# A two-layer kernel (routed experts, then a gated recurrence): fp32 injection of the gate inputs on TensorE, output sum on VectorE, GpSimd left with scaling

## The chip, the cores and the metric

The kernel runs on one NeuronCore of a Trainium2 chip. The metric is the device time of one execution, in microseconds (us). Five engines work side by side: TensorE (PE in the rows, its weight loads PEld), VectorE (DVE), ScalarE (ACT), GpSimd (POOL) and SyncE (SP), which only issues transfers here.

## What is computed

The input x is (2, 1024, 256): B = 2 sequences, T = 1024 steps, D = 256 features. The first layer is a mixture of four experts and a shared branch, the second a gated recurrence over the 1024 steps. Both add to their input.

```python
# layer 1, per expert e (and the shared branch), weights w_be from a small gating network
h = gelu(x @ ew1[e] + eb1[e]);  y = h @ ew2[e] + eb2[e]
out = out + w_be[:, e] * mask[e] * y          # H = 1024 hidden units
x = x + out + shared(x)
# layer 2, with v* = cond @ C_* + b_*
def step(h, xs):                               # 1024 times, each needs the h before it
    z = sigmoid(xzt + h @ U_z + vz)
    r = sigmoid(xrt + h @ U_r + vr)
    hh = tanh(xht + r * h @ U + vh)
    return (1.0 - z) * h + z * hh
x = x + all h                                  # xz, xr, xh = x @ W_z, x @ W_r, x @ W
```

## The kernel before

Everything lies features on partitions (two blocks of 128, KC = 2) and time and batch along the free side. Time is cut into CH = 16 chunks of TC = 64 steps, each chunk into BODIES = 4 bodies of STEPS = 16 steps: 64 bodies, counted n = 0 to 63, with steps t = 0 to 15 in each.

**The recurrence.** One step (`gru_body` on TensorE and on VectorE) goes round three engines. TensorE multiplies the state by the recurrent matrices, cut into fp16 halves (`u_high`, `u_mid`), with the state in fp16 halves as well (`h_parts`, HI and LO): 8 products on HI and 4 on LO for gate R, the same for Z (all at L873). ScalarE takes the tanh of R (`gate_tanh`, L481), VectorE forms r*h in halves (`p_parts`, L684 to L687), TensorE multiplies these for the candidate C (8 and 4 products again), ScalarE takes its tanh, and VectorE's scans (L701 to L705) make the new state, the fp16 HI half first, then LO (L708). The rest of the R products waits for LO.

**The side work.** Layer 1 of later chunks runs on TensorE in two windows of every step: window 0 between the Z products and the C products, window 1 after the C products (`gap_work`). A table (`UNITS`) gives window 0 one unit and window 1 two, and only one to window 1 where t is 7 or 15. A unit is one fp32 product, a weight matrix of 128x128 on 128 columns (`up` L806, `down` L822, `gate_input` L833): two MATMUL records in the trace. Where the table has no unit, `gap_work` issues bf16 products that are not used (L887): one of 256 columns in window 0, two of 512 in window 1. ScalarE applies the gelu (L476), and GpSimd multiplies the result by the expert's weight (`scale_tile`, L298), for which `down` waits.

**The injection.** A PSUM bank per gate holds the inputs of a whole body: at its start `inject` writes the projected inputs of 16 steps (64 columns) into the bank, and the recurrent products add to them. Projected inputs are made by `gate_input` and ScalarE (`input_part`, L491) into `xpart`, fp32. GpSimd then cuts `xpart` into three bf16 parts (`split`, L372 to L379), and `inject` multiplies each on a bf16 identity (L859): three products for a gate. Gate R of body n+1 is injected at the end of body n after window 1 of t = 15, gate Z at t = 0 between R's HI and R's LO products (in other steps three of Z's HI products stand there), gate C at t = 0 ahead of window 0.

```python
def inject(g, last_of_body):
    for i in range(3):
        last = mm(gate_ps[g][:, 0:KC * SC], ident16[:, :],
                  xsplit[:, i, g * KC:(g + 1) * KC, :].rearrange("p k n -> p (k n)"),
                  start=(i == 0), stop=(i == 2), skip_group_check=True)
```

**The output.** At the end of a body VectorE marks it (L712), GpSimd scales the 16 states (L387) and adds the layer's input (`add_body`, L392) into `out_feat`; TensorE transposes the sum to rows in window 1 of t = 1 of the next body (`turn_body`, L854; in body 0 it turns zeros), ScalarE copies them out (L500, after t = 5), SyncE stores.

Of the kernel before, what the change touches and what calls it, by code (L numbers as in the profile page):

```python
# [23 lines left out]
ALU = mybir.AluOpType  # L24
# [4 lines left out]
BF16 = mybir.dt.bfloat16  # L29
I32 = mybir.dt.int32  # L30

P = 128
# [17 lines left out]
def moe_gru_kernel(nc, x, cond, gate_w, gate_b, time_w, time_b, ew1, eb1, ew2, eb2, sw1, sb1, sw2, sb2,  # L50
# [45 lines left out]
    UNITS, GELUS, RESIDUALS, PIECES, FIRST_SPLIT = {}, {}, {}, {}, {}  # L96
    for c in range(CH - 1):
        slots = [(c * TC + s, window) for s in range(TC)
                 for window in ((0, 1) if s % 8 == 7 else (0, 1, 1))]
        for kind, f, i in side_work(c):  # L100
# [13 lines left out]
            if kind == PROJECT:  # L114
                after = at[0] + at[1]
                for m in range(KC):
                    PIECES[after + m] = [(f, i, m, b) for b in range(B)]
                FIRST_SPLIT[after + KC] = f
    FIRST_SPLIT = {max(step for step, g in FIRST_SPLIT.items() if g == f): f for f in range(1, CH)}
# [6 lines left out]
    with ctx:  # L126
# [30 lines left out]
        xrest = sb("xrest", [P, GATES * KC, SC])  # L157
        xsplit = sb("xsplit", [P, 3, GATES * KC, SC], BF16)
        h_hist = sb("h_hist", [P, ROUND, 2 * ST])
        h_true = sb("h_true", [P, KC, SC])  # L160
# [35 lines left out]
        body_mark = sb("body_mark", [P, 1])  # L196
# [35 lines left out]
        pool_passed = sem("pool_passed")  # L232
# [29 lines left out]
        split_ready = sem("split_ready")  # L262
# [7 lines left out]
        body_h = sem("body_h")  # L270
        body_added = sem("body_added")
        h_unscaled = sem("h_unscaled")
# [29 lines left out]
        def _(sp):  # L302
# [6 lines left out]
            sp.sem_inc(out_written, 2 * 16)  # L309

# [12 lines left out]
            def store_body(n):  # L323

                sp.wait_ge(turned_copied, n + 2)
# [14 lines left out]
            sp.wait_ge(out_written, (CH * BODIES + 1) * 2 * 16)  # L340
# [3 lines left out]
        def _(pool):  # L344
# [10 lines left out]
            pool.sem_inc(split_ready, 1)  # L355
            pool.memset(out_feat[:, :, :], 0.0).then_inc(body_added, 1)
            CHAIN0, PER_SPLIT = 1, 3

            def wait_apart(semaphore, value):

                pool.wait_ge(semaphore, value)
                pool.sem_inc(pool_passed, 1)

            def split(c, j):

                n = c * BODIES + j
                chain = n * PER_SPLIT + CHAIN0
                src = xpart[:, c % 2, :, j * SC:(j + 1) * SC]
                if j == 0:
                    pool.wait_ge(xp_ready, (c + 1) * (GATES * KC * B) + 1)  # L370
                wait_apart(injected, n + 1)
                pool.tensor_copy(xsplit[:, 0, :, :], src).then_inc(pool_chain, 1)  # L372
                wait_apart(pool_chain, chain + 1)
                pool.tensor_tensor(xrest[:, :, :], src, xsplit[:, 0, :, :],
                                   ALU.subtract).then_inc(pool_chain, 1)
                wait_apart(pool_chain, chain + 2)
                pool.tensor_copy(xsplit[:, 1, :, :], xrest[:, :, :]).then_inc(pool_chain, 1)
                pool.wait_ge(pool_chain, chain + 3)
                pool.tensor_tensor(xsplit[:, 2, :, :], xrest[:, :, :], xsplit[:, 1, :, :],  # L379
                                   ALU.subtract).then_inc(split_ready, 1)  # L380

            def add_body(n):

                first = n % 2 * STEPS
                wait_apart(body_h, n + 1)
                for k in range(KC):
                    pool.tensor_scalar(h_true[:, k, :].rearrange("p (s b) -> p s b", b=B),  # L387
                                       h_now[:, first:first + STEPS, k * B:(k + 1) * B],
                                       h_unscale[:, :], None, ALU.mult).then_inc(h_unscaled, 1)
                wait_apart(h_unscaled, KC * (n + 3))  # L390
                wait_apart(turned, n + 1)
# [583 lines left out]
```

## Time and profile before

| | |
|---|---|
| median of 3 runs | 2120.41 us (2115.2, 2120.41, 2125.93) |
| the profiled execution's own time | 2111.95 us |
| its span | 2110.1 us |
| granted TensorE clock over the span | 0.995 of full speed |
| PE busy / PEld busy | 2069.1 us (98%) / 1817.8 us (86%) |
| DVE, ACT, POOL busy | 1201.6 (57%), 732.4 (35%), 395.9 us (19%) |
| first and last of the 1024 state scans (L701) | 85.9 us, 2104.1 us |

So 86 us go before the recurrence, 2018 us into its steps, 6 us behind them. The profile counts as busy every engine that has an instruction in flight; with matmuls pipelined, 98% does not say that TensorE could take nothing more. The span is read from the first to the last instruction, and the execution's own time is 1.9 us longer.

### The profile page before, as it was taken

Reading aid. Unit: us, or ns where it says so; the run is one execution under the profiler, and the core shown is the slowest. Engines: PE = TensorE matmul, PEld = TensorE weight load, DVE = VectorE, ACT = ScalarE, POOL = GpSimd, SP = SyncE. Lnnn points to the kernel's source line nnn. Section 1 sums busy time; section 2 is a strip of 40 time slices with the busy share of each in tenths; the row PEclk is TensorE's granted clock in tenths of the full one; section 3 lists DMA queues with packets and bytes.
Section 4 is the critical chain, followed back from the end, with each engine's and each line's share of the span. In section 5 each row is a group of like instructions: output and inputs, shape, how many; then the busy total and the mean of one; then the engine's idle time right before and its main releaser. Section 6 shows DMA issues by size and latency. Waiting matters only on the chain.

```text
span 2110.1 us, 105994 instructions
## 1 busy us (share of the span) xinstructions
PE 2069.1 (98%) x43624; PEld 1817.8 (86%) x43624; DVE 1201.6 (57%) x10446; ACT 732.4 (35%) x3977; POOL 395.9 (19%) x931
## 2 busy tenths in 40 slices
PE   7999999999999999999999999999999999999998
PEld 6998988989888898988888888898988889888665
DVE  6455555555555555555555555555555555555555
ACT  2433333333333333333333333333333333333222
POOL 3121212121121211212122121211212122120010
PEclk8999999999999999999999999999999999999999
DMA  8000000000000000000000000000000000000000
GB/s 285 2 4 5 5 4 5 4 4 5 5 4 5 5 4 5 5 4 5 5 4 4 5 4 4 4 4 4 5 5 4 5 4 4 5 5 4 4 4 4
DMA packets 16931, 23.90 MB, mean 11 GB/s; under 512 B 3584, under 2 KB 15159, under 8 KB 16444
## 3 DMA queue, kind: packets, MB, share of 16 engines
q1 hardware_dynamic: 15280, 17.05, 2.5%
q8 instruction: 341, 5.59, 1.1%
q14 instruction: 146, 1.20, 0.2%
q10 hardware_dynamic: 1164, 0.07, 0.0%
HBM read 15.01 MB, written 2.10 MB: 8 GB/s over the span
## 4 chain that ended last, share of the span: by engine, by line
PE 94%; issue 2%; DVE 2%; ACT 1%; POOL 0%; POOLq 0%; DVEq 0%; ACTq 0%
PE c_ps L873 21%; PE r_ps L873 19%; PE y_ps L822 17%; PE up_ps L806 17%; PE z_ps L873 14%; PE xp_ps L833 2%; PE up_ps L887 2%; PE xp_ps L887 1%; DVE p_parts L684 1%; ACT r_ps L481 1%; PE rows_ps L854 1%; DVE h_parts L701 1%; DVE hidden L298 0%; ACT c_ps L481 0%; PE y_ps L795 0%
## 5 line engine op out<-in xcount | busy, mean ns | idle before, releaser
L873 PE MATMUL z_ps<-h_parts,u_high 128*128 128x20 f16 x8192 | 566.6, 178 | 0.0
L873 PE MATMUL r_ps<-h_parts,u_high 128*128 128x20 f16 (+1 forms) x8192 | 545.8, 172 | 10.4 <-DVE h_parts L701 0.2
L873 PEld LDWEIGHTS r_ps<-h_parts,u_high 128*128 128x128 f16 x8192 | 419.6, 96 | 154.9 <-DVE h_parts L701 86.3
L873 PE MATMUL c_ps<-p_parts,u_high 128*128 128x56 f16 (+1 forms) x8192 | 532.0, 178 | 11.0
L822 PE MATMUL y_ps<-hidden,down_w 128*128 128x128 f32 x2560 | 524.9, 301 | 4.5 <-DVE hidden L298 4.5
L806 PE MATMUL up_ps<-feat,up_w 128*128 128x128 f32 x2560 | 527.1, 302 | 0.0
L873 PEld LDWEIGHTS c_ps<-p_parts,u_high 128*128 128x128 f16 x8192 | 418.3, 96 | 106.5 <-DVE p_parts L684 33.6
L684 DVE SCALAR_TENSOR_TENSOR p_parts<-r_ps,h_hist 128x4 f16<-128x4 f32 x1024 | 168.4, 164 | 483.8 <-ACT r_ps L481 483.8
L873 PE MATMUL z_ps<-h_parts,u_mid 128*128 128x20 f16 x4096 | 438.3, 178 | 0.0
L873 PEld LDWEIGHTS z_ps<-h_parts,u_high 128*128 128x128 f16 x8192 | 423.5, 95 | 0.0
L481 ACT ACTIVATE r_ps<-r_ps 128x4 f32<-128x4 f32 x1024 | 161.8, 158 | 640.0 <-PE r_ps L873 636.1
L701 DVE TENSOR_TENSOR_SCAN h_parts<-c_ps,blend 128x8 f16<-128x8 f32 x1024 | 178.2, 174 | 344.7 <-ACT c_ps L481 340.4
L822 PEld LDWEIGHTS y_ps<-hidden,down_w 128*128 128x128 f32 x2560 | 367.2, 190 | 5.9 <-issue 3.4
L806 PEld LDWEIGHTS up_ps<-feat,up_w 128*128 128x128 f32 x2560 | 369.5, 191 | 0.4 <-issue 0.2
L481 ACT ACTIVATE c_ps<-c_ps 128x4 f32<-128x4 f32 x1024 | 161.8, 158 | 584.4 <-PE c_ps L873 584.4
L873 PE MATMUL c_ps<-p_parts,u_mid 128*128 128x56 f16 x4096 | 350.2, 187 | 0.0
L873 PE MATMUL r_ps<-h_parts,u_mid 128*128 128x20 f16 x4096 | 336.6, 178 | 0.0
L873 PEld LDWEIGHTS z_ps<-h_parts,u_mid 128*128 128x128 f16 x4096 | 295.6, 96 | 0.0
L873 PEld LDWEIGHTS c_ps<-p_parts,u_mid 128*128 128x128 f16 x4096 | 260.7, 96 | 0.7
L873 PEld LDWEIGHTS r_ps<-h_parts,u_mid 128*128 128x128 f16 x4096 | 256.5, 97 | 0.0
L476 ACT ACTIVATE hidden<-up_ps,small_cols 128x128 f32<-128x128 f32 x640 | 234.5, 366 | 41.0 <-PE up_ps L806 39.9
L690 DVE TENSOR_SCALAR blend<-z_ps,half_s 128x4 f32<-128x4 f32 x1024 | 218.9, 214 | 0.0
(137 smaller groups left out, 2274.8 us busy)
## 6 DMA issues: line engine op xcount, KB each, us to landing
up_w<-in_L_cond_ew SPq DMA_DIRECT2D x4, 1024.0 KB, 12.0
down_w<-in_L_cond_ew SPq DMA_DIRECT2D x4, 1024.0 KB, 13.2
x_rows<-in_x SPq DMA_DIRECT2D x8, 256.0 KB, 5.1
out<-out_rows SPq DMA_DIRECT2D x128, 16.0 KB, 1.8
up_w<-in_L_cond_sw SPq DMA_DIRECT2D x1, 1024.0 KB, 15.7
down_w<-in_L_cond_sw SPq DMA_DIRECT2D x1, 1024.0 KB, 11.8
cf<-in_L_cond_C_r SPq DMA_DIRECT2D x1, 256.0 KB, 5.9
cf<-in_L_cond_C_z SPq DMA_DIRECT2D x1, 256.0 KB, 6.1
```

The lines of the kernel that those rows point to most:

```text
L476: act.activation(hidden[:, i % LAG, :], up_ps[i % 2][:, 0:COLS], ACT.Gelu_apprx_tanh, bias=small_cols[:, ROW_B1 + e * HT + j:ROW_B1 + e * ...
L481: act.activation((c_now, tanh_r, tanh_z)[(g + 1) % GATES].rearrange("p (m b) -> p m b", b=B), gate_v[g][:, :, step % STEPS, :], ACT.Tanh, ...
L684: dve.scalar_tensor_tensor(p(HI), tr, 1.0, prev, ALU.add, ALU.mult).then_inc(part_ready, 1)
L690: dve.tensor_scalar(blend_v[:, :, 0], tz, 1.0, half_s[:, :], ALU.add, ALU.mult).then_inc(state, 1)
L701: dve.tensor_tensor_scan(h_parts[:, HI, 0, :], cand, blend[:, :], 0.0, ALU.mult, ALU.add).then_inc(part_ready, 1)
L806: last = mm(up_ps[i % 2][:, 0:COLS], up_w[:, e, k, j * P:(j + 1) * P], feat[:, k, f * COLS:(f + 1) * COLS], start=(k == 0), stop=(k == KC ...
L822: last = mm(y_ps[:, m * COLS:(m + 1) * COLS], down_w[:, e, j, m * P:(m + 1) * P], hidden[:, i % LAG, :], start=False, stop=(m == KC - 1), ...
L833: last = mm(xp_ps[:, m * COLS:(m + 1) * COLS], wx[:, g, k, m * P:(m + 1) * P], feat[:, k, f * COLS:(f + 1) * COLS], start=(m == 0 and k == 0),
L854: last = pe.transpose(rows_ps[0:SC, k * P:(k + 1) * P], out_feat[:, k, :], ident[:, :])
L873: return mm(gate_ps[g][:, m * SC + t * B:m * SC + t * B + width], w[:, g, k, m * P:(m + 1) * P], moving, start=False, stop=i == LO and k = ...
L887: mm(idle_ps[:, 0:IDLE_FILL[window]], ident16[:, :], keep_warm[:, 0:IDLE_FILL[window]], start=True, stop=True, skip_group_check=True)
```

## The change

GpSimd no longer cuts the projected inputs, nor sums the output rows. `inject` makes one fp32 product per gate of `xpart` itself on the fp32 identity. Two VectorE instructions per body (`output`, one per block of features, at t = 2 and t = 3 of the next body, behind `blend`) scale the states and add the layer's input; both their tensors lie in SBUF. The transposes move from t = 1 to t = 5 of the next body, the row copy from t = 5 to t = 8; the transposes of zeros go. The marks, the semaphores and the buffers of the old paths go too.

```diff
-            def split(c, j):
-                n = c * BODIES + j
...
-                pool.tensor_copy(xsplit[:, 0, :, :], src).then_inc(pool_chain, 1)
...
-                pool.tensor_tensor(xsplit[:, 2, :, :], xrest[:, :, :], xsplit[:, 1, :, :],
-                                   ALU.subtract).then_inc(split_ready, 1)
-            def add_body(n):
-                first = n % 2 * STEPS
-                wait_apart(body_h, n + 1)
...
-                wait_apart(turned, n + 1)
-                pool.tensor_tensor(out_feat[:, :, :], h_true[:, :, :],
-                                   feat[:, :, n * SC:(n + 1) * SC], ALU.add
-                                   ).then_inc(body_added, 1)
...
             for step in range(T):
-                n, t = divmod(step, STEPS)
-                c, j = divmod(n, BODIES)
-                if t == 0 and n > 0:
-                    add_body(n - 1)
-                if t == 3 and j < BODIES - 1:
-                    split(c, j + 1)
-                if step in FIRST_SPLIT:
-                    split(FIRST_SPLIT[step], 0)
                 for f, i in GELUS.get(step, ()):
                     if i < SCALED:
                         scale_tile(pool, f, i)
-            add_body(CH * BODIES - 1)
...
                     act.wait_ge(xp_done, c * GATES + (g + 1))
-                    if g == 0:
-                        act.wait_ge(split_ready, max(c - 1, 0) * BODIES + 1)
+                    if g == 0 and c >= 2:
+                        act.wait_ge(injected, (c - 1) * BODIES)
...
-                if step % STEPS == 5:
-                    copy_rows(step // STEPS)
+                if step % STEPS == 8 and step > STEPS:
+                    copy_rows(step // STEPS - 1)
...
+            def output(n, k):
+
+                half = n % 2 * STEPS
+                if k == 0:
+                    dve.wait_ge(turned, n)
+                dve.scalar_tensor_tensor(out_feat[:, k, :].rearrange("p (s b) -> p s b", b=B),
+                                         h_now[:, half:half + STEPS, k * B:(k + 1) * B], h_unscale[:, :],
+                                         feat[:, k, n * SC:(n + 1) * SC].rearrange("p (s b) -> p s b", b=B),
+                                         ALU.mult, ALU.add).then_inc(body_added, 1)
...
                         residual(*RESIDUALS[first + t])
+                    if n > 0 and 2 <= t < 2 + KC:
+                        output(n - 1, t - 2)
 
                     dve.wait_ge(act_done, gate0 + 3)
                     dve.wait_ge(state, s0 + 3)
-                    if t == 0:
-                        dve.wait_ge(h_unscaled, KC * (n + 1))
...
-                    if t == STEPS - 1:
-                        dve.memset(body_mark[:, :], 0.0).then_inc(body_h, 1)
...
+            dve.wait_ge(state, (T + 1) * STATE_STEP)
+            for k in range(KC):
+                output(CH * BODIES - 1, k)
...
-                pe.wait_ge(body_added, n + 1)
+                pe.wait_ge(body_added, KC * (n + 1))
+                pe.wait_ge(turned_copied, n)
                 for k in range(KC):
...
-            def inject(g, last_of_body):
-                for i in range(3):
-                    last = mm(gate_ps[g][:, 0:KC * SC], ident16[:, :],
-                              xsplit[:, i, g * KC:(g + 1) * KC, :].rearrange("p k n -> p (k n)"),
-                              start=(i == 0), stop=(i == 2), skip_group_check=True)
-                if last_of_body:
+            def inject(g, n):
+
+                c, j = divmod(n, BODIES)
+                if g == R and j == 0:
+                    pe.wait_ge(xp_ready, (c + 1) * (GATES * KC * B) + 1)
+                last = mm(gate_ps[g][:, 0:KC * SC], ident[:, :],
+                          xpart[:, c % 2, g * KC:(g + 1) * KC, j * SC:(j + 1) * SC],
+                          start=True, stop=True, skip_group_check=True)
+                if g == C:
                     last.then_inc(injected, 1)
...
-                if t == 1 and window == 1:
-                    turn_body(n)
+                if t == 5 and window == 1 and n > 0:
+                    turn_body(n - 1)
...
                     if t == STEPS - 1 and not last:
-                        pe.wait_ge(split_ready, n + 3)
-                        inject(R, False)
+                        inject(R, n + 1)
...
-            turn_body(CH * BODIES)
+            turn_body(CH * BODIES - 1)
```

How the instructions stand now, first TensorE from the end of body 0 to the start of body 1, before:

```order
L873 MATMUL c_ps<-p_parts,u_high 128x2 x4
L822 MATMUL y_ps<-hidden,down_w 128x128
L859 MATMUL r_ps<-xsplit,ident 128x64 x3
L873 MATMUL r_ps<-h_parts,u_high 128x20
...
L859 MATMUL z_ps<-xsplit,ident 128x64 x3
L873 MATMUL r_ps<-h_parts,u_high 128x2 x4
...
L859 MATMUL c_ps<-xsplit,ident 128x64 x3
L806 MATMUL up_ps<-feat,up_w 128x128
L873 MATMUL c_ps<-p_parts,u_high 128x56
```

and in the changed kernel:

```order
L821 MATMUL c_ps<-p_parts,u_high 128x2 x4
L766 MATMUL y_ps<-hidden,down_w 128x128
L807 MATMUL r_ps<-xpart,ident 128x64
L821 MATMUL r_ps<-h_parts,u_high 128x20
...
L807 MATMUL z_ps<-xpart,ident 128x64
L821 MATMUL r_ps<-h_parts,u_high 128x2 x4
...
L807 MATMUL c_ps<-xpart,ident 128x64
L750 MATMUL up_ps<-feat,up_w 128x128
L821 MATMUL c_ps<-p_parts,u_high 128x56
```

Each run of three bf16 products has become one fp32 product in the same place. The second place is VectorE at t = 2 and 3 of body 1, in the changed kernel (`out_feat` is the sum for the output):

```order
L632 TENSOR_TENSOR p_parts<-r_ps,p_parts 128x2x2
L635 TENSOR_SCALAR blend<-z_ps,half_s 128x4
L636 SCALAR_TENSOR_TENSOR blend<-z_ps,half_h 128x4
L612 SCALAR_TENSOR_TENSOR out_feat<-h_hist,h_unscale,feat 128x32
L646 SCALAR_TENSOR_TENSOR h_parts<-c_ps,blend 128x8
```

The row with `out_feat` is new there; before, the scan into `h_parts` followed `blend` directly.

## Rows read from the trace of the kernel before

**Rows 1.** The page, part 4: the chain that ended last, share of the span by engine.

```profile
PE 94%; issue 2%; DVE 2%; ACT 1%; POOL 0%; POOLq 0%; DVEq 0%; ACTq 0%
```

**Rows 2.** The waits: engine, line <- released by: us in total, times, longest us.

```profile
DVE h_parts L701 <- ACT c_ps L481: 340.4, 994, 0.5
PEld r_ps L873 <- DVE h_parts L701: 86.3, 230, 0.5
...
PEld rows_ps L854 <- POOL out_feat L392: 2.4, 1, 2.4
```

**Rows 3.** Timeline of PE around the start of body 32: start us, us, engine line op.

```profile
1093.86 0.59 PE L887 MATMUL xp_ps<-keep_warm,ident 128*128 128x512 bf16 x2
1094.29 0.25 PE L859 MATMUL r_ps<-xsplit,ident 128*128 128x64 bf16 x3
1094.45 0.18 PE L873 MATMUL r_ps<-h_parts,u_high 128*128 128x20 f16 x1
...
1094.67 0.25 PE L859 MATMUL z_ps<-xsplit,ident 128*128 128x64 bf16 x3
1094.75 0.24 PE L873 MATMUL r_ps<-h_parts,u_high 128*128 128x2 f16 x4
...
1095.16 0.25 PE L859 MATMUL c_ps<-xsplit,ident 128*128 128x64 bf16 x3
1095.24 0.47 PE L822 MATMUL y_ps<-hidden,down_w 128*128 128x128 f32 x2
1095.54 0.19 PE L873 MATMUL c_ps<-p_parts,u_high 128*128 128x56 f16 x1
```

**Rows 4.** Timeline of PE, body 33, t = 1, window 1: transposes, then two units.

```profile
1129.67 0.61 PE L806 MATMUL up_ps<-feat,up_w 128*128 128x128 f32 x4
1130.11 0.18 PE L873 MATMUL r_ps<-h_parts,u_high 128*128 128x20 f16 x1
```

**Rows 5.** Timeline of PE, end of body 33, with a unit in window 1.

```profile
1157.02 0.47 PE L806 MATMUL up_ps<-feat,up_w 128*128 128x128 f32 x2
...
1157.62 0.18 PE L873 MATMUL r_ps<-h_parts,u_high 128*128 128x20 f16 x1
```

**Rows 6.** Timeline of PE, start of body 63 (last chunk: no units).

```profile
2073.59 0.25 PE L859 MATMUL c_ps<-xsplit,ident 128*128 128x64 bf16 x3
2073.67 0.27 PE L887 MATMUL up_ps<-keep_warm,ident 128*128 128x256 bf16 x1
2073.88 0.20 PE L873 MATMUL c_ps<-p_parts,u_high 128*128 128x56 f16 x1
```

**Rows 7.** Groups of lines: TensorE's 12 fp32 products on 2 columns.

```profile
L779 PE MATMUL r_ps<-small_cols,cf 128*128 128x2 f32 x24 | 5.3, 354 | 0.0
```

**Rows 8.** The stretch 18 to 22 us: busy us by engine, then PEclk.

```profile
18.00:22.00 4.00, 4.00 (x20) 4.00 (x20) 2.90 (x19) 1.49 (x2) 0.00 (x0) 0.50 1.06 383
```

**Rows 9.** Timeline without PE, a step at t = 2.

```profile
1130.14 0.40 POOL L298 TENSOR_TENSOR hidden<-hidden,expert_w 128x128 f32<-128x128 f32 x1 [2.22 <-ACT hidden L476]
...
1131.34 0.15 DVE L691 SCALAR_TENSOR_TENSOR blend<-z_ps,half_h 128x4 f32<-128x4 f32 x1
...
1131.83 0.17 DVE L701 TENSOR_TENSOR_SCAN h_parts<-c_ps,blend 128x8 f16<-128x8 f32 x1 [0.34 <-ACT c_ps L481]
```

**Rows 10.** Timeline of VectorE and GpSimd in the setup.

```profile
35.88 0.29 DVE L298 TENSOR_TENSOR hidden<-hidden,expert_w 128x128 f32<-128x128 f32 x1 [0.60 <-ACT hidden L476]
...
36.75 5.46 POOL L406 TENSOR_SCALAR uf<-uf,w_scale 128x1536 f32<-128x1536 f32 x1 [7.34 <-issue]
36.77 4.88 DVE L298 TENSOR_TENSOR hidden<-hidden,gate_scale 128x128 f32<-128x128 f32 x4 [0.60 <-ACT hidden L476]
```

**Rows 11.** Timeline, the end of the program.

```profile
2104.49 0.15 DVE L710 TENSOR_SCALAR half_h<-c_ps 128x4 f32<-128x4 f32 x1
...
2106.23 0.61 PE L854 MATMUL rows_ps<-ident,out_feat 128*32 128x128 f32 x2 [1.88 <-POOL out_feat L392]
```

More of the change, by code:

```diff
@@ L94, in side_work @@
         return work + [item for some in later[3:] for item in some]
-    UNITS, GELUS, RESIDUALS, PIECES, FIRST_SPLIT = {}, {}, {}, {}, {}
+    UNITS, GELUS, RESIDUALS, PIECES = {}, {}, {}, {}
     for c in range(CH - 1):
@@ L117, in moe_gru_kernel @@
                     PIECES[after + m] = [(f, i, m, b) for b in range(B)]
-                FIRST_SPLIT[after + KC] = f
-    FIRST_SPLIT = {max(step for step, g in FIRST_SPLIT.items() if g == f): f for f in range(1, CH)}
     ROW_B1, ROW_BG, ROW_COND = 0, BR * HT, BR * HT + GATES * KC
@@ L231, in moe_gru_kernel @@
         pool_chain = sem("pool_chain")
-        pool_passed = sem("pool_passed")
         x_turned = sem("x_turned")
@@ L261, in moe_gru_kernel @@
         xp_ready = sem("xp_ready")
-        split_ready = sem("split_ready")
         injected = sem("injected")
@@ L307, in _ @@
                                  ).then_inc(x_in[i], 16)
-            sp.sem_inc(out_written, 2 * 16)
             def load_expert(e):
@@ L323, in store_body @@
             def store_body(n):
-                sp.wait_ge(turned_copied, n + 2)
+                sp.wait_ge(turned_copied, n + 1)
                 for b in range(B):
@@ L339, in _ @@
                 store_body(n)
-            sp.wait_ge(out_written, (CH * BODIES + 1) * 2 * 16)
+            sp.wait_ge(out_written, CH * BODIES * 2 * 16)
         @block.gpsimd
@@ L354, in _ @@
                                       bass.bass_isa.ReduceOp.max).then_inc(umax_shared, 1)
[L355 to L362, printed above, removed]
-            def split(c, j):
-                n = c * BODIES + j
[L367 to L371, printed above, removed]
-                pool.tensor_copy(xsplit[:, 0, :, :], src).then_inc(pool_chain, 1)
[L373 to L378, printed above, removed]
-                pool.tensor_tensor(xsplit[:, 2, :, :], xrest[:, :, :], xsplit[:, 1, :, :],
-                                   ALU.subtract).then_inc(split_ready, 1)
-            def add_body(n):
-                first = n % 2 * STEPS
-                wait_apart(body_h, n + 1)
[L386 to L390, printed above, removed]
-                wait_apart(turned, n + 1)
-                pool.tensor_tensor(out_feat[:, :, :], h_true[:, :, :],
-                                   feat[:, :, n * SC:(n + 1) * SC], ALU.add
-                                   ).then_inc(body_added, 1)
             pool.wait_ge(expert_w_made, 1)
@@ L525, in _ @@
                     gelu(f, i)
-                if step % STEPS == 5:
-                    copy_rows(step // STEPS)
+                if step % STEPS == 8 and step > STEPS:
+                    copy_rows(step // STEPS - 1)
                 for piece in PIECES.get(step, ()):
                     input_part(*piece)
-            copy_rows(CH * BODIES)
+            copy_rows(CH * BODIES - 1)
         @block.vector
@@ L547, in _ @@
             dve.memset(h_hist[:, :, :], 0.0)
-            dve.sem_inc(h_unscaled, 2 * KC)
             dve.memset(cand, 0.0)
@@ L729, in _ @@
             mm = pe.matmul
-            pe.sem_inc(injected, 1)
             pe.wait_ge(ident_made, 3)
@@ L898, in gru_body @@
                     if t == 0:
-                        inject(Z, False)
+                        inject(Z, n)
                     early = 0 if t == 0 else 3
@@ L913, in gru_body @@
                         pe.wait_ge(state, (n * STEPS + 1) * STATE_STEP)
-                        inject(C, True)
+                        inject(C, n)
                     gap_work(n, t, 0)
@@ L940, in _ @@
             pe.wait_ge(gbias_made, 1)
-            pe.wait_ge(split_ready, 2)
-            inject(R, False)
+            inject(R, 0)
             for n in range(CH * BODIES):
                 gru_body(n, n == CH * BODIES - 1)
-            turn_body(CH * BODIES)
+            turn_body(CH * BODIES - 1)
 _INS = ['x', 'cond_1024', 'L0_cond_gate_w', 'L0_cond_gate_b', 'L0_cond_time_w', 'L0_cond_time_b',
```

8 lines of the change are left out of this document (removed).

## The prediction

> **What bounds the kernel now.** I read the chain of waits first, then the waits by pair, then TensorE's timeline where one body passes into the next.
>
> The chain that ended last lies on TensorE for 94% [rows 1]. That alone would say that TensorE has no room. The waits correct it: VectorE's scan stands idle 340.4 us for ScalarE's tanh of C, 994 times, and TensorE's weight loads for R stand 86.3 us for VectorE's new state, 230 times [rows 2]. So a step is a round trip over three engines, and TensorE's side work fills the two windows of the round trip almost to the brim. The scans run from 85.9 to 2104.1 us, over 1023 steps 1.973 us each. A product added to TensorE is free only where a window has room left; one added between the products of a gate is paid in full.
>
> GpSimd is on no such path: the only wait of TensorE for it in the list of the waits is one of 2.4 us at the end of the program [rows 2]. Its 396 us of busy time (19%) hide under the recurrence, so taking work from it gives nothing back except at that end. So the question is what the three injections cost.
>
> **What three bf16 products cost.** At the start of body 32 [rows 3], Z's three start at 1094.67 and R's LO products at 1094.75; C's start at 1095.16 and the next unit at 1095.24. That is 0.08 us for each gate.
>
> **What one fp32 product on 64 columns costs.** No row has it, so I bound it. On 128 columns, between fp16 products, a unit starts at 1095.24 and C's products at 1095.54: 0.30 us [rows 3]. Behind another fp32 product it is less: the four records (two units) from 1129.67 to 1130.11 take 0.22 us a unit [rows 4]. On 2 columns, 12 fp32 products took 5.3 us [rows 7], 0.44 us each, at a granted clock of 0.50 [rows 8]: 0.22 us at full clock. So 128 columns and 2 columns cost the same once the products follow one another; what is paid is not the columns but the loading of the 128 weight columns, several times over. Fewer columns can shorten only the last stretch of an isolated product. Two fillers of 512 columns take 0.43 us (1093.86 to 1094.29, [rows 3]), 0.42 ns for a column, so 64 columns fewer are worth 0.03 us at the end. I take 0.27 us alone between fp16 products, and 0.22 us next to another fp32 product; the ends are 0.22 and 0.30. Over the bf16 form: 0.19 us more (0.14 to 0.22).
>
> **Gate Z.** Its injection stands between R's HI and R's LO products. LO has to wait for VectorE anyway, but TensorE comes to it only just in time: the LO products follow the injection without a gap [rows 3]. All 0.19 us go to the round trip, in 64 bodies: 12.2 us.
>
> **Gate C.** Its injection and one unit stand in window 0. Before: 0.08 + 0.30 = 0.38 us. After: two fp32 products behind each other, 0.30 + 0.22 = 0.52 us. C's products already start directly behind the unit [rows 3], so nothing absorbs the difference: 0.14 us in the 59 bodies whose table has a unit there, 8.3 us. In the last five there is a filler instead: C's injection at 2073.59, filler at 2073.67, C's products at 2073.88 [rows 6]. With 0.27 and 0.11 for half of a filler of 512 columns they could start at 2073.97: 0.09 late, 0.4 us in all.
>
> **Gate R.** Its injection ends window 1 of t = 15, which holds only one unit. At the end of body 33 the unit starts at 1157.02 and R's products, released by the scan, at 1157.62 [rows 5]: 0.60 us. Unit and fp32 injection need 0.52. It fits, nothing is paid in 44 bodies. In 19 bodies the table has no unit there (the last body of each of 14 chunks, and bodies 58 to 62) and two fillers of 512 columns take its place: 1093.86 + 0.43 + 0.27 = 1094.56, against 1094.45 now [rows 3], 0.11 us late. R's HI products, the injection of Z and the LO products then follow back to back, so it stays: 19 x 0.11 = 2.1 us.
>
> **The transposes** move from window 1 of t = 1 to window 1 of t = 5, each with two units beside them in either place (fillers in the last chunk): no change, and one turn fewer in the loop, under 0.1 us. The row copy moves from behind t = 5 to behind t = 8 on ScalarE, where it stands behind the gelu at most, as it does now.
>
> **VectorE's two sums** (128x32) go where VectorE idles. At t = 2 `blend` ends at 1131.49 and the scan starts at 1131.83 [rows 9]: 0.34 us free. The sum's price lies between `blend`'s 0.15 us (4 columns, [rows 9]) and 0.29 us for a sum of two SBUF tensors on 128 columns [rows 10]; even the upper end fits. Cost nothing, hidden under ScalarE's tanh of C and the C products ahead of it; without that cover it would be 128 x 0.19 = 24 us. The mark of 0.06 us and the waits for it go, off the path.
>
> One rule speaks against this placement. First the row: in the setup four VectorE products of two SBUF tensors took 4.88 us together beside a GpSimd operation of 5.46 us, one alone 0.29 us [rows 10]. The Trainium skill, page "SBUF — State Buffer", section "SBUF: two separate sides", says that VectorE and GpSimd hold a shared port pair for a whole instruction, and that a VectorE operation with two SBUF inputs is shut out by a GpSimd operation that reads SBUF; the trace agrees. But in the loop GpSimd's scaling runs at 1130.14 for 0.40 us, behind the previous scan, and is over at 1130.54, 0.80 us before `blend` starts at 1131.34 [rows 9]. They do not meet. That is a rival below.
>
> **The end.** From `half_h` (ends 2104.64) to the last transposes (2106.23) GpSimd's scaling, its waits and its sum take 1.59 us [rows 11]. Two VectorE instructions with one hop between engines need some 0.5 us: 1.1 us gained.
>
> **Sum**: 12.2 + 8.3 + 0.4 + 2.1 - 1.1 = 21.9 us slower. Against the profiled execution's own 2111.95 us that gives 2133.9 us. The three runs have their median 8.5 us higher, at 2120.41 us, and I set the sum on that: 2142 us, 1.0% slower.
>
> **Rivals.**
> *The columns are the price.* If the weight loads were hidden, an fp32 product on 64 columns would cost half of the 0.22 us of 128 columns, 0.11 us, 0.03 us more than now. Z: 64 x 0.03 = 1.9 us; C: 59 x 0.03 = 1.8 us; R nothing; the end -1.1 us: 2.6 us, 2123 us, not slower in a measurement (what can be told from no change here is 0.5%, 10.6 us). It decides below some 0.17 us for the product. Against it stand the 2-column products [rows 7, 8]. The Trainium skill, page "FP8 and Floating Point Precision", section "TensorE Precision Notes", counts four passes for true fp32. By it alone four passes of 64 columns stand against three, a third more than now, and the time would be this rival's. 7%.
> *VectorE's sum is shut out by GpSimd.* If the scaling ran late enough to meet it, the sum would wait up to 0.40 us and take 0.19: 0.25 us over its free 0.34 us, in up to 128 steps, 32 us: 2174 us. Only steps with a scaling could pay, and the 0.80 us between them speak against it. 4%.
> *The first weight load hides* under the fp16 products ahead, so that every fp32 product costs 0.22: Z 64 x 0.14 = 9.0, C 59 x 0.06 = 3.5, R 19 x 0.06 = 1.1, less 1.1: 12.5 us, 2133 us. Against it stands the 0.30 us of a unit between fp16 products. 12%; it lies inside my range.
> *Gain from freeing GpSimd.* It would need a wait for it in the loop; there is none. 2%.
>
> **Numbers.** The forecast has 75%. With 0.30 us for a product and no saving from its length, Z costs 14.1, C 59 x 0.22 = 13.0, R 19 x 0.14 = 2.7: with the end, 28.7 us, 2149 us. The range runs from the hidden load to this, and 2 us further down for the scatter of the runs: 2131 to 2150 us. Slower by over 0.5% (above 2131 us): the forecast, the late sum and nearly all of the hidden load, 0.90. Within 0.5%: 0.08. Faster: 0.02.
>
> **What will show it.** An fp32 injection on L807 with 0.27 us from its start to R's LO products; C's products 0.52 us behind C's injection; steps at t = 0 some 0.33 us longer than now, the other steps as now, except that what the transposes cost moves from t = 2 to t = 6; the sums behind `blend` at 0.2 us each, and the scans at t = 2 and 3 on time. If R's LO products follow Z's injection after 0.11 us, the price was the columns. If steps at t = 2 and 3 grow, it was VectorE's sum.

## The result and the profile after

The changed kernel takes 2166.43 us (median of 4 runs, 2155.67 to 2175.46) where the kernel before, run beside it, takes 2122.23 us (4 runs, 2115.2 to 2125.93). The ratio is 1.021, with a 95% interval of 1.0154 to 1.0266. The direction was forecast, the size was not: 44 us instead of 22, and the median lies 16 us above the range's upper end.

The profiled execution took 2175.46 us, the longest of the four, against 2111.95 us for that of before. The page of the changed kernel, parts 1, 2 and 4 (busy time of each engine; granted clock in 40 slices; shares of the chain that ended last):

```profile
span 2173.7 us, 104824 instructions
PE 2130.4 (98%) x43359; PEld 1890.8 (87%) x43430; DVE 1221.6 (56%) x10510; ACT 737.1 (34%) x3976; POOL 218.0 (10%) x482
PEclk8999989989899999989999999898999999899999
PE 95%; DVE 3%; ACT 1%; issue 1%; POOL 0%; DVEq 0%; ACTq 0%
```

GpSimd has lost 178 us of work, and the chain is as it was [rows 1]. The third line is what I had not asked about. Before, its mean over the span was 0.995; now it is 0.962, and seven slices behind the first show an 8.

**What the products cost.** TensorE's timeline at the start of body 33 of the changed kernel (start us, us, engine, line, operation; these answer to [rows 3]):

```profile
1161.81 0.47 PE L766 MATMUL y_ps<-hidden,down_w 128*128 128x128 f32 x2
1162.11 0.33 PE L807 MATMUL r_ps<-xpart,ident 128*128 128x64 f32 x2
1162.40 0.18 PE L821 MATMUL r_ps<-h_parts,u_high 128*128 128x20 f16 x1
...
1162.62 0.41 PE L807 MATMUL z_ps<-xpart,ident 128*128 128x64 f32 x2
1162.87 0.24 PE L821 MATMUL r_ps<-h_parts,u_high 128*128 128x2 f16 x4
...
1163.27 0.41 PE L807 MATMUL c_ps<-xpart,ident 128*128 128x64 f32 x2
1163.52 0.44 PE L750 MATMUL up_ps<-feat,up_w 128*128 128x128 f32 x2
1163.80 0.19 PE L821 MATMUL c_ps<-p_parts,u_high 128*128 128x56 f16 x1
```

Z's injection takes 0.25 us (1162.62 to 1162.87) where three bf16 products took 0.08: 0.17 more. C's and its unit take 0.53 (1163.27 to 1163.80) where it was 0.38: 0.15 more. Over all bodies with a unit there (up to body 58) and outside the slow stretches described below, worked out from the starts of the scans, the median step at t = 0 is 2304 ns instead of 1997. Of the 307, 167 lie between the last scan and the tanh of R (Z's product) and 140 between r*h and the tanh of C. In the last five bodies it is 167 in all, all of it Z's.

**VectorE's sum and the end** (timeline without TensorE's own products at t = 2 of body 33, then the end of the program):

```profile
1166.77 0.40 POOL L289 TENSOR_TENSOR hidden<-hidden,expert_w 128x128 f32<-128x128 f32 x1 [3.81 <-ACT hidden L412]
...
1167.91 0.15 DVE L636 SCALAR_TENSOR_TENSOR blend<-z_ps,half_h 128x4 f32<-128x4 f32 x1
1167.98 0.24 DVE L612 SCALAR_TENSOR_TENSOR out_feat<-h_hist,h_unscale,feat 128x32 f32<-128x32 f32 x1
...
1168.41 0.17 DVE L646 TENSOR_TENSOR_SCAN h_parts<-c_ps,blend 128x8 f16<-128x8 f32 x1 [0.18 <-ACT c_ps L417]
...
2169.34 0.15 DVE L655 TENSOR_SCALAR half_h<-c_ps 128x4 f32<-128x4 f32 x1
2169.53 0.41 DVE L612 SCALAR_TENSOR_TENSOR out_feat<-h_hist,h_unscale,feat 128x32 f32<-128x32 f32 x2
2170.00 0.39 PE L799 MATMUL rows_ps<-ident,out_feat 128*32 128x128 f32 x2 [0.80 <-DVE out_feat L612]
```

The sum takes 0.24 us, begins 0.81 us after GpSimd has ended, and leaves 0.18 us before the scan, which still waits for ScalarE; the scan comes 1.97 us after the one before it (which starts at 1166.44), on time. Over the whole program no sum meets a scaling: the closest follows 0.76 us behind one. At the end the transposes start 0.51 us behind `half_h` instead of 1.59.

**Where the rest went.** Busy time and granted clock of the changed kernel in four stretches around the passage from body 6 to body 7 (columns: stretch, its length, busy us and instructions of PE, PEld, DVE, ACT, POOL, then the granted clock, DMA share, GB/s):

```profile
290.00:302.70 12.70, 12.43 (x269) 10.33 (x267) 7.73 (x67) 4.27 (x24) 1.20 (x3) 1.00 0.02 5
302.70:305.60 2.90, 2.90 (x59) 2.58 (x55) 1.64 (x15) 1.50 (x8) 0.00 (x0) 1.00 0.03 8
305.60:322.70 17.10, 17.10 (x253) 16.35 (x250) 7.06 (x63) 4.55 (x25) 1.03 (x3) 0.50 0.01 2
322.70:335.00 12.30, 12.17 (x267) 10.98 (x266) 6.73 (x60) 4.83 (x26) 1.49 (x4) 1.00 0.03 7
```

And two successive scans inside the third stretch, from VectorE's timeline:

```profile
308.28 0.17 DVE L646 TENSOR_TENSOR_SCAN h_parts<-c_ps,blend 128x8 f16<-128x8 f32 x1 [1.21 <-ACT c_ps L417]
311.05 0.17 DVE L646 TENSOR_TENSOR_SCAN h_parts<-c_ps,blend 128x8 f16<-128x8 f32 x1 [0.70 <-ACT c_ps L417]
```

For 17.1 us the clock is granted at half, the lower of its two levels (1.2 instead of 2.4 GHz), and a step takes 2.77 us instead of 1.97. PE counts as fully busy all the while, so its busy share says nothing of it. Such a stretch is called a fall below. Only those inside the recurrence count: every profile, that of before too, has a stretch at half clock in the setup (as in [rows 8]) and one behind the last scan. There are eleven falls, from 6.8 to 20.5 us long, 150 us together; by the lengths of their steps they cost 47 us. Each begins within 1.5 us of the start of the fourth body of a chunk (bodies 7, 11, 15 to 43, and 55). The profile of before shows none, but its runs beside the experiments below point to them: their mean clocks lie between 0.975 and 0.996, and in batch 2 three runs at 0.996 took 2112 to 2113 us, three at 0.988 took 2120 to 2123.

What TensorE did just before the fall at 305.6, at t = 14 of the third body (its timeline, changed kernel):

```profile
302.54 0.25 PE L821 MATMUL c_ps<-p_parts,u_high 128*128 128x2 f16 x4
302.72 0.71 PE L739 MATMUL y_ps<-branch_rows,bias_rows 5*128 5x128 f32 x4
303.36 0.18 PE L821 MATMUL r_ps<-h_parts,u_high 128*128 128x20 f16 x1
```

These are the bias products (`output_bias`): the expert biases times the branch weights, two fp32 products on only 5 of the 128 rows. They fill this window in the third body of 14 chunks, bodies 2, 6 and so on to 54, and 11 of the 14 are followed by a fall. A window with a single unit and the start of the next body come behind them. They stand there in both kernels (L795 before). The place is the same wherever a profile of this study shows falls: 94 of them in ten profiles, and each begins 0.7 to 3.3 us after the start of the last of these bias products.

**The sum of the profiles.** 59 x 0.307 + 5 x 0.167 = 18.9 us of products, 47 us of falls, 1.25 us less behind the last scan, 1.8 us less before the first (from 82.7 to 86.1 us in the runs of this study, without pattern): 62.9 us, against 63.6 us between the spans. This is the longest of the four executions; the median lost less to falls.

### The profile page after: what moved, and what is told of

Its sections match the earlier page's. It is cut to its first block, busy times and chain, and to the rows that moved or that the text cites. A ratio compares the mean times of both kernels' runs of the same rounds, so it can differ in the third digit from the quotient of the medians.

```text
span 2173.7 us, 104824 instructions
## 1 busy us (share of the span) xinstructions
PE 2130.4 (98%) x43359; PEld 1890.8 (87%) x43430; DVE 1221.6 (56%) x10510; ACT 737.1 (34%) x3976; POOL 218.0 (10%) x482
## 4 chain that ended last, share of the span: by engine, by line
PE 95%; DVE 3%; ACT 1%; issue 1%; POOL 0%; DVEq 0%; ACTq 0%
PE c_ps L821 20%; PE r_ps L821 18%; PE y_ps L766 17%; PE up_ps L750 17%; PE z_ps L821 14%; PE xp_ps L777 3%; PE up_ps L835 2%; PE xp_ps L835 1%; DVE p_parts L629 1%; ACT r_ps L417 1%; PE c_ps L807 1%; PE z_ps L807 1%; PE rows_ps L799 1%; PE r_ps L807 1%; DVE h_parts L646 1%
## 5 line engine op out<-in xcount | busy, mean ns | idle before, releaser
L821 PEld LDWEIGHTS r_ps<-h_parts,u_high 128*128 128x128 f16 x8192 | 434.1, 97 | 146.6 <-DVE h_parts L646 77.7
L821 PE MATMUL r_ps<-h_parts,u_high 128*128 128x20 f16 (+1 forms) x8192 | 551.4, 173 | 8.3
L821 PE MATMUL c_ps<-p_parts,u_high 128*128 128x56 f16 (+1 forms) x8192 | 541.7, 180 | 10.9
L750 PE MATMUL up_ps<-feat,up_w 128*128 128x128 f32 x2560 | 540.3, 308 | 0.0
L766 PE MATMUL y_ps<-hidden,down_w 128*128 128x128 f32 x2560 | 534.8, 306 | 4.3 <-DVE hidden L289 4.3
L821 PEld LDWEIGHTS c_ps<-p_parts,u_high 128*128 128x128 f16 x8192 | 432.5, 97 | 102.7 <-DVE p_parts L629 33.6
L750 PEld LDWEIGHTS up_ps<-feat,up_w 128*128 128x128 f32 x2560 | 379.6, 196 | 0.4 <-issue 0.2
L766 PEld LDWEIGHTS y_ps<-hidden,down_w 128*128 128x128 f32 x2560 | 374.4, 194 | 5.7 <-DVE hidden L289 4.2
L821 PE MATMUL c_ps<-p_parts,u_mid 128*128 128x56 f16 x4096 | 359.3, 189 | 0.0
L821 PEld LDWEIGHTS c_ps<-p_parts,u_mid 128*128 128x128 f16 x4096 | 270.3, 98 | 4.0
```

Source lines behind the costliest of these rows:

```text
L750: last = mm(up_ps[i % 2][:, 0:COLS], up_w[:, e, k, j * P:(j + 1) * P], feat[:, k, f * COLS:(f + 1) * COLS], start=(k == 0), stop=(k == KC ...
L766: last = mm(y_ps[:, m * COLS:(m + 1) * COLS], down_w[:, e, j, m * P:(m + 1) * P], hidden[:, i % LAG, :], start=False, stop=(m == KC - 1), ...
L821: return mm(gate_ps[g][:, m * SC + t * B:m * SC + t * B + width], w[:, g, k, m * P:(m + 1) * P], moving, start=False, stop=i == LO and k = ...
```

## The experiments

The questions were whether the clock's falls, not the products, are the missing half, what starts them, and which part of the change makes them worse. My theory before these runs: around the passage from the third to the fourth body TensorE's work is thin because of the 5-row products, and the slower body start tips it over or holds it down. The rivals: the output path (moved transposes) does it; the longer body alone does it; the fp32 product for R at the body's end does it. In the diffs, "before" and "after" name the kernel that the edit starts from; every line without + or - is context.

**Batch 1** (four kernels on one chip; before 2127.37 us beside them, mean clocks 0.975 to 0.985).

*Injection only*: before, with the fp32 product for all gates; GpSimd goes on cutting, and the output path is the old one.

```diff
             def inject(g, last_of_body, n):
-                for i in range(3):
-                    last = mm(..., ident16[:, :], xsplit...)
+                c, j = divmod(n, BODIES)
+                last = mm(gate_ps[g][:, 0:KC * SC], ident[:, :],
+                          xpart[:, c % 2, g * KC:(g + 1) * KC, j * SC:(j + 1) * SC], ...)
```

> The kernel before, with the fp32 injection for all three gates and nothing else moved (GpSimd still cuts, its parts unused; it still sums the output). If the injections are the whole cause, steady bodies take 31.85 us as in the changed kernel (31.53 before), the granted clock falls to 0.50 in most third-to-fourth-body passages, and the time is about 2167 us. If the falls come from the moved transposes, the moved row copy or VectorE's sums, there are none here, and the time is 2120 + 20 = 2140 us.

2151.42 us (4 runs, 2146.27 to 2151.97), ratio 1.0104 (1.0077 to 1.0131), between the two times that were expected. The step at t = 0 is 2304 ns, as in the changed kernel. The profile has eleven falls, mostly 6.8 us long, so they need nothing of the new output path. (The edit also makes ScalarE wait until `xpart` has been injected before it writes there again.)

*Output path only*: after, with GpSimd's `split` and three bf16 products.

```diff
+            def split(c, j): ...                     # on GpSimd, as before
             def inject(g, n):
-                last = mm(..., ident[:, :], xpart..., start=True, stop=True)
+                for i in range(3):
+                    last = mm(..., ident16[:, :], xsplit[:, i, ...], ...)
```

> The changed kernel's output path (VectorE's sums, transposes at t = 5, row copy at t = 8) with the old three bf16 products and GpSimd's cutting. If the injections are the whole cause: no falls of the clock, bodies of 31.53 us, 1 us below the kernel before by the shorter end. If the output path brings the falls: over 2150 us.

2129.19 us (10 runs), ratio 1.0001 (0.9979 to 1.0024): the output path is free within 0.2%, as forecast. But there are seven falls in its profile too, 3.4 to 20.5 us long, where none was expected if the fp32 injection were the whole cause. So falls do not need the fp32 injection.

*Longer bodies*: before, with the bf16 products of Z and C issued three times each.

```diff
-                        inject(Z, False)
+                        for _ in range(3):
+                            inject(Z, False)
```

> The kernel before, with Z's and C's three bf16 injection products issued three times over (the first two times are overwritten), so the body is longer by about as much as with fp32 (0.17 + 0.17 us), but by bf16 products only. Theory A, the fp32 product itself lets the clock fall (its array waits for weights): no falls, about 2120 + 20 = 2140 us. Theory B, the passage from the third to the fourth body of a chunk was thin before too, and any longer body only shifts it against the moments at which the chip decides: falls here too, 2150 to 2170 us.

2135.17 us (9 runs), ratio 1.0037 (1.0023 to 1.0051). Its step at t = 0 is 2347 ns, a little longer than with fp32; seven falls, each only 3.4 us. It stands 8 us above the kernel before, though its steps at t = 0 alone are some 22 us longer (64 x 0.35): with the extra bf16 products it loses less to falls than before did beside it.

*Full rows*: after, with the bias products on 128 rows, 123 of them zeros.

```diff
-        bias2_rows = sb("bias2_rows", [BR, D])
+        bias2_rows = sb("bias2_rows", [P, D])
-        branch_rows = sb("branch_rows", [BR, T * B])
+        branch_rows = sb("branch_rows", [P, T * B])
+            pool.memset(bias2_rows[:, :], 0.0)       # and branch_rows, before they are filled
```

> The changed kernel, with the products of the output bias (L739 of it, 5 rows, at t = 14 of each third body, just ahead of the falls) on 128 rows filled up with zeros. If these few-row products are what makes the passage thin, no falls or few, 2120 + 17 = 2137 us, and the 0.1 us that t = 15 of these bodies takes more is gone as well. If the fp32 injections alone do it: falls as before, about 2165 us.

2126.55 us (10 runs, 2124.34 to 2127.17), ratio 0.9994 (0.998 to 1.0008); clock 0.995, no fall. The 2137 us expected were set on before's median, and so held before's own falls. The products still cost their 307 ns at t = 0. So the falls are the missing half, and they hang on the 5-row products; batch 3 has both kernels on one chip. TensorE's timeline of this kernel in the same place:

```profile
303.95 0.25 PE L826 MATMUL c_ps<-p_parts,u_high 128*128 128x2 f16 x4
304.06 0.69 PE L744 MATMUL y_ps<-branch_rows,bias_rows 128*128 128x128 f32 x4
304.66 0.18 PE L826 MATMUL r_ps<-h_parts,u_high 128*128 128x20 f16 x1
```

With 5 rows the bias products start 0.18 us behind the start of C's last four; with 128, 0.11 us. So two things changed, the rows and a short gap. The 64-row run below parts them.

**Batch 2** (before 2116.37 us, clocks 0.988 to 0.996).

*Before with full rows*: the edit of *full rows* on before.

> The kernel before, with the output-bias products on 128 rows filled up with zeros, nothing else. If the kernel before loses its clock at the few-row products too (its runs here show a mean granted clock of 0.975 to 0.985), this removes it: granted clock 0.995 and over, 2108 to 2112 us, 0.8% below before. If before has no such loss, the same time as before but for the 15 x 0.1 us at t = 15.

2108.02 us (6 runs, 2107.53 to 2108.62), ratio 0.9955 (0.994 to 0.997), no fall. So before, too, loses by these products, 8.4 us here. Not all of it is clock: before's own runs at 0.996 took 2112 to 2113 us, which leaves some 4 us of its median to falls. Another 1.4 us are 14 steps at t = 15 of the third bodies, which take 2.07 us behind 5 rows and 1.97 behind 128. What the rest is, some 3 us, no run shows.

*Output path and full rows*: the edits of *output path only* and of *full rows* together (bf16 injection, VectorE's sums, 128 rows).

> Bf16 injection cut by GpSimd, VectorE's output sums, and bias products on 128 rows: everything that proved good. Expected 1 us below the run with the kernel before and 128 rows alone, about 2109 us; against the changed kernel with 128 rows (2126.5) it prices the fp32 injection without any fall of the clock: 59 x 0.31 + 5 x 0.17 = 19 us less. If the injection's price were only the clock, this would be equal to 2126 us.

2107.2 us (5 runs, 2106.71 to 2108.47), ratio 0.9953 (0.9933 to 0.9972). With *before with full rows*, which it equals within their scatter, it beats both kernels of this study.

*fp32 for R alone*: before, with the fp32 product for one gate.

```diff
+                if g == R:
+                    last = mm(gate_ps[g][:, 0:KC * SC], ident[:, :], xpart..., start=True, stop=True)
-                for i in range(3):
+                for i in range(0 if g == R else 3):
```

> The kernel before with the fp32 injection for gate R alone, which lies at the end of t = 15, in the thin passage, and costs no time (the window has room), so bodies keep 31.53 us and their place against the chip's decisions. If the fp32 product itself thins the passage: more or longer falls than before, granted clock under 0.975, 2135 us and over. If only the length of the bodies and the few-row products count: as before, 2127 us.

2117.49 us (10 runs, 2109.93 to 2125.04), ratio 0.9999 (0.998 to 1.0018). The bodies' steps are unchanged, and it has seven falls of 3.4 to 6.8 us. The fp32 product at the body's end neither costs nor makes the falls worse by an amount these runs can tell.

*Z in halves*: after with full rows, Z's fp32 product cut into two of 32 columns: the same columns, twice the products.

```diff
+                for k in range(KC) if g == Z else [slice(0, KC)]:
+                    last = mm(gate_ps[g][:, k * SC:(k + 1) * SC], ident[:, :],
+                              xpart[:, c % 2, g * KC + k, j * SC:(j + 1) * SC], ...)
```

> The changed kernel with bias products on 128 rows, and Z injected by two fp32 products on 32 columns instead of one on 64. If the loading of the 128 weight columns is the price, each product more costs 0.22 us in every body: 64 x 0.22 = 14 us over the 2126.5 us of the same kernel with one product. If streamed columns are the price: no difference.

2140.28 us (4 runs, 2139.22 to 2140.5), ratio 1.0104 (1.0081 to 1.0126), 13.7 us more than *full rows* of batch 1. Its timeline at the start of a body:

```profile
1140.05 0.52 PEld L814 LDWEIGHTS z_ps<-xpart,ident 128*128 128x128 f32 x4
1140.07 0.61 PE L814 MATMUL z_ps<-xpart,ident 128*128 128x32 f32 x4
1140.52 0.24 PE L830 MATMUL r_ps<-h_parts,u_high 128*128 128x2 f16 x4
```

Z takes 0.45 us instead of 0.25, with no column more. The Trainium skill, page "FP8 and Floating Point Precision", section "TensorE Precision Notes", counts four passes for true fp32; by passes and columns alone this edit would be free. It cost 0.20 us a body, so on so few columns the measurement decides against the columns: the price goes by the product. That it is the weight loads is read from the trace: the four of Z fill 0.52 us (1140.05 to 1140.57), 0.19 us each with overlaps. On one chip, this kernel less *output path and full rows* is 33.1 us; less the 64 x 0.196 = 12.5 us of the second Z product (scan to tanh of R, 975 to 1171 ns) that leaves 20.5 us for the fp32 form and the rest, close to the 18.9 us read from the steps. Neither kernel has a fall.

**Batch 3** (before 2124.95 us, clocks 0.976 to 0.987). *Injection only* had come out 15 us below the changed kernel, but on another chip. So both, and the cure, on one:

> The changed kernel once more, on the same chip as the next three, so that the falls of the clock are priced on one chip: about 2166 us, granted clock 0.96 to 0.98.

> The changed kernel with the bias products on 128 rows, on the same chip: 2126 us again, granted clock 0.995 and over. The difference to the changed kernel beside it is the price of the falls: 40 us expected.

> The kernel before with the fp32 injection alone, on the same chip as the changed kernel. It had 2151 us where the changed kernel had 2166 on another chip. If the moved output path makes the falls longer (transposes of 32 weight columns at t = 5, inside the stretch in which the clock would have to come back), the changed kernel is some 15 us slower here too; if that was the chip, the two agree.

The changed kernel: 2160.19 us (4 runs), ratio 1.0166 (1.0123 to 1.021), clock 0.972 in its profile. Full rows: 2126.14 us (10 runs), ratio 1.0006 (0.999 to 1.0021), clock 0.996. Injection only: 2158.18 us (4 runs), ratio 1.0162 (1.0123 to 1.0202), clock 0.978. The full-row kernel in the stretch in which the changed kernel lay at half clock in the result's profile (columns as above):

```profile
305.60:322.70 17.10, 16.97 (x367) 15.41 (x366) 10.08 (x90) 7.04 (x38) 1.60 (x4) 1.00 0.01 3
```

367 PE instructions instead of 253 in the same 17.1 us. The 5-row products cost the changed kernel 34 us on this chip (2160.19 - 2126.14). The steps of its profile say the same: its eight falls, 6.8 to 17.1 us long, cost 33 us, and 1.4 us go to t = 15. The injection alone loses as much as the whole change, within the scatter of the runs.

*Transposes later*: the changed kernel, with the transposes at t = 9 and the row copy behind t = 12.

```diff
-                if t == 5 and window == 1 and n > 0:
+                if t == 9 and window == 1 and n > 0:
```

> The changed kernel with the transposes at t = 9 and the row copy behind t = 12, nothing else. If the transposes at t = 5 keep the clock from coming back, the falls end at t = 2 or 3 and the time is 10 to 15 us below the changed kernel beside it. If not, the same time.

2155.32 us, but from 2138.38 to 2185.97 in 4 runs (clocks 0.952 to 0.988); without the longest the ratio is 1.0118 (1.0056 to 1.018). The transposes' 47 ns went to t = 10 as they should. On the falls it says nothing: their lengths reach 27 us in its profile, which is that of the longest run, and the scatter is wider than any difference that I looked for.

**Batch 4** (before 2123.8 us, clocks 0.984 to 0.992).

*64 rows*: *full rows* with half of the rows.

```diff
-        bias2_rows = sb("bias2_rows", [P, D])
+        bias2_rows = sb("bias2_rows", [64, D])       # and branch_rows
```

> The changed kernel with the bias products on 64 rows filled up with zeros, not 128. If the share of the array's rows in use is what counts, falls come back in part: between 2126 and 2160 us, granted clock between 0.97 and 0.995. If it is the gap of 0.09 us before and behind a product of fewer rows, and the gap is still there at 64, it is as the changed kernel, 2160 us; if 64 rows are enough, 2126 us with no falls.

2129.3 us (10 runs, 2126.86 to 2130.83), ratio 1.003 (1.0018 to 1.0041), clock 0.996, no fall. The place of the bias products:

```profile
302.33 0.25 PE L826 MATMUL c_ps<-p_parts,u_high 128*128 128x2 f16 x4
302.51 0.71 PE L744 MATMUL y_ps<-branch_rows,bias_rows 64*128 64x128 f32 x4
303.15 0.18 PE L826 MATMUL r_ps<-h_parts,u_high 128*128 128x20 f16 x1
```

The gap of 0.18 us is back to the hundredth, and the falls stay away. So it is the few rows, not the gap. This kernel stands 3.2 us above full rows of batch 3, on another chip; its steps at t = 15 of the third bodies are 0.1 us longer than theirs, 1.4 us in 14 bodies, and the rest I did not find. In the six profiles with 64 or 128 rows there is no fall, and all 45 runs of these kernels have a mean clock of 0.995 to 0.998.

*Much longer bodies*: before, with the bf16 products of Z and C five times, beside *injection only* once more.

```diff
-                        inject(Z, False)
+                        for _ in range(5):
+                            inject(Z, False)
```

> The kernel before with Z's and C's bf16 injection products five times over: bodies longer by 0.7 us, by bf16 products only. If the falls depend on length alone, they may be as many and as long as with the fp32 injection: granted clock 0.975, and over 20 us above the sum 2118 + 64 x 0.65 = 2160 us. If it is the fp32 product that lengthens them, they end as early as with three times over (3.4 us each, granted clock 0.99): 2160 to 2170 us.

> The kernel before with the fp32 injection alone, beside the two others on one chip: 2151 to 2158 us, granted clock 0.975 to 0.98, falls of 6.8 us and more.

Much longer bodies: 2161.98 us (4 runs), ratio 1.0181 (1.0162 to 1.02). Injection only: 2159.22 us (4 runs), ratio 1.0173 (1.0151 to 1.0195). A fall of the one, then one of the other (columns as above):

```profile
301.00:308.30 7.30, 7.20 (x156) 6.02 (x153) 4.15 (x36) 2.30 (x15) 0.13 (x1) 1.00 0.01 2
308.30:311.70 3.40, 3.40 (x67) 3.23 (x65) 1.13 (x11) 0.78 (x5) 1.03 (x3) 0.50 0.03 7
311.70:318.00 6.30, 6.30 (x140) 5.84 (x138) 3.36 (x30) 2.16 (x13) 0.40 (x1) 1.00 0.01 3
```

```profile
560.00:566.70 6.70, 6.70 (x150) 6.11 (x146) 3.42 (x33) 2.46 (x14) 0.42 (x2) 1.00 0.01 4
566.70:573.60 6.90, 6.90 (x101) 6.53 (x98) 2.83 (x25) 1.38 (x8) 0.99 (x3) 0.51 0.01 2
573.60:580.00 6.40, 6.40 (x140) 5.86 (x137) 3.36 (x30) 2.72 (x16) 0.40 (x1) 1.00 0.01 3
```

About as many falls (ten and eleven), but all of 3.4 us in the one and of 6.8 to 10.2 in the other; by their steps they cost 11 and 27 us. The step at t = 0 is 2697 ns in the one and 2304 in the other. The rival of mere length falls: starts of bodies that are longer by twice as much lose less than half to falls. With the same output path, fp32 products instead of more bf16 ones go with longer falls, in this batch and against *longer bodies*. Beside the kernel before itself the injection alone costs 24, 33 and 35 us on three chips, where its steps explain 18.9: so 5 to 17 us come on top, most likely falls (in this batch its clocks are 0.974 to 0.976 against 0.984 to 0.992 for before). But the extra bf16 products may also shorten them, and bf16 kernels have longer ones too (up to 6.8 us in *fp32 for R alone*, 20.5 in *output path only*). Why a fall lasts as long as it does, no run shows.

## Why the prediction was right and wrong

- **Gate Z**: right in its mechanism. 0.19 us was forecast, 0.17 measured, paid in the round trip in full. 10.7 us (64 x 0.167) for 12.2.
- **Gate C**: right. 0.14 and 0.140. In the last five bodies, with a filler, nothing was paid where I had 0.09 each; the step there is longer by Z's 0.167 alone.
- **Gate R**: the term of 2.1 us was wrong. Behind a filler of 512 columns the fp32 product takes 0.17 us, not 0.27, so it is hidden in all bodies: R's products start 0.23 us behind the scan (2073.97), as in other steps. TensorE's timeline at the start of body 63 of the changed kernel:

```profile
2073.60 0.59 PE L835 MATMUL up_ps<-keep_warm,ident 128*128 128x512 bf16 x2
2074.03 0.33 PE L807 MATMUL r_ps<-xpart,ident 128*128 128x64 f32 x2
2074.20 0.18 PE L821 MATMUL r_ps<-h_parts,u_high 128*128 128x20 f16 x1
```

- **VectorE's sums, the transposes, the end**: right. 0.24 us hidden under ScalarE's tanh of C, the 0.05 us moved from t = 2 to t = 6 (2013 to 1967 and 1967 to 2014 ns), and 1.25 us gained for 1.1. By the rule of the Trainium skill, page "SBUF — State Buffer", section "SBUF: two separate sides", GpSimd could have shut VectorE out; the two did not meet, with 0.76 us or more between them. *Output path only* shows what a meeting costs: there GpSimd cuts again, and 29 of the 128 sums start during its subtraction of two SBUF tensors. Each ends some 0.05 us behind it, and 15 of them take 0.29 to 0.31 us instead of 0.24, still inside their free 0.34 us.
- **The price of the product**: not the columns, as argued from [rows 7, 8] and now shown by *Z in halves*; that it is the weight loads is read from their rows. The rivals *the columns are the price* and *VectorE's sum is shut out* are out. *The first weight load hides* holds behind fillers of 512 columns only; behind fp16 products the 0.25 us lie between its 0.22 and my 0.27.
- **The step that failed**: the sum. It took every duration from a profile at 0.995 of full clock and assumed that the changed kernel would be granted the same: there was no term and no rival for the clock. With the clock kept (*full rows*) the change costs the steps' 18.9 us less the end's 1.25, some 17.7 us for the 21.9 of my sum; between the two full-row kernels, on two chips, lie 18.1 us (2126.14 - 2108.02). The 44 us between the medians leave 26 us more to falls than before had. Before had some 10 itself (2122.23 less the 2111.95 of its execution without falls), so the changed kernel lost some 37 us to them, and 33 in batch 3.
- The profile alone could not have shown this, for it had no fall; the runs could. Their median lay 8.5 us above the profiled execution, and I set the sum on the median without asking what those 8.5 us were. The clocks of those three runs are not on record, but the same gap stands between before's runs at 0.996 and at 0.988 in batch 2: falls, most likely. So the place was already on the edge, and it stands next to the very bodies' starts that the change made longer.

Left open: why the 5-row products bring the clock down, and why the fp32 injection adds to what is lost. It is also open whether the moved transposes have a part in it. In the four profiles with the new output path and falls the longest takes 17.1 to 27.3 us, in the six without that path never more than 10.2; yet in batch 3 the times agree. No run explains some 3 us of *before with full rows* and the 1.8 us before the first scan.

## What to carry to other kernels

Ask of every run, not only of the profiled one, what clock it was granted: a profiled execution that is some tenths of a per cent faster than the median may be the one that was spared, and a sum made from it leaves the most sensitive place out. Matmuls on a few rows amid small products were such a place here; zeros up to 128 rows cost nothing in the loop and were worth 0.45% to the kernel before and 34 us to the changed one. And price an fp32 product on few columns by the product, not by its columns: 0.25 us alone against 0.08 us for three bf16 products of 64 columns, while work taken from an engine on no path (178 us of GpSimd's) gives back nothing but 1.25 us at the end.

## What was unexpected of the hardware

- At half clock a step loses less than half of its speed: at 0.50 a step takes 2.77 us instead of 1.97, and VectorE's scan takes 0.17 us at either clock.
- Rows of zeros are enough: with 123 or 59 of them beside the 5 of data, no profile shows a fall in the recurrence, and no run has a mean clock under 0.995.
- An fp32 product of 64 columns takes 0.17 us behind a stream of 512 columns and 0.25 us behind fp16 products; two with half the columns each take 0.45.
- Fewer rows than 128 cost a gap: the bias products start 0.07 us later with 5 or with 64 rows than with 128.
